# A routed-expert kernel: batch registers of the last group loaded earlier, additions chained by twos

## The chip, the cores and the metric

The kernel runs on one core of one Trainium2 chip. The metric is the device time of the kernel in microseconds; lower is better. Before the change three runs took 675.02, 675.02 and 675.72 us.

## What is computed

The reference has two residual stages on x, of shape 64 batches x 64 steps x 256 features, all in float32.

```python
x = x + _L0_cond_ref(x, cond, weight, bias)     # a gated recurrent cell, scanned over the 64 steps
x = x + _L1_cond_ref(x, cond, ...)              # a gated mixture of 4 experts, 2 for each batch

for e in range(E):                              # E = 4
    h = gelu(context_c @ ew1[e] + eb1[e])       # 256 -> 1024
    y = h @ ew2[e] + eb2[e]                     # 1024 -> 256
    out = out + w_be[:, e][:, None, None] * mask[e][None, :, None] * y
shared = gelu(context_c @ sw1 + sb1) @ sw2 + sb2
return out + shared
```

`w_be` is zero for the two experts that a batch did not choose. The mask takes steps 21 to 41 out of expert 1 and steps 0 to 20 out of expert 2. Which expert a batch goes to is known only while the kernel runs.

## The kernel before

**Stages.** The recurrent scan runs step by step; beside it TensorE works on the shared expert in groups of 8 steps (512 columns). When the scan is over, the gate is computed (`gate_means` to `gate_weights`), and from it two lists: `slot_b`, one row of batch numbers on partition 0, and `slot_w`, the weights. A group of the routed part takes 8 slots (experts 0 and 3, 64 steps each, 512 columns) or 10 slots (expert 1: 44 steps that are used, 440 columns, with step 21 set to zero by a memset; expert 2: 43 steps, 430 columns). Every group has 10 places in the list (`WIDE`). Places without a batch hold batch 0 with weight 0. Expert q of `ORDER` has groups `sv[q]` to `sv[q+1]`, with `sv` read from the chip (`group_bounds`); each expert has one group at least. With these inputs there are 15 groups: seven for expert 0 (from 348 us), one for expert 3 (from 498), six for expert 1 (from 520), one for expert 2 (from 635).

**One group.** Eight chunks of 128 hidden units. For each one TensorE does layer 1 (`hp`), ScalarE the gelu (L364, `g_f`) and the rounded copy (L369, `g_hi`), DVE the rest `g_lo = g_f - g_hi` (L458, `split_lo`), TensorE layer 2 (`zy`) with `g_hi` and, last, with `g_lo`. Layer 2 of chunk j comes behind layer 1 of chunk j + 2. Layer 2 of the last two chunks is interleaved with layer 1 of the next group (`turnover`). Every matmul is recorded at L775.

**What DVE does beside it.** When a group's layer 2 is complete, `weigh` (L671) adds the bias, multiplies by the slots' weights and writes `y_w`. During the next group `add_slots` loads batch numbers into registers (L686), two or three at a time, and adds each slot's part of `y_w` into `acc` at the address of its batch (L692). Each addition waits until the one before is complete: empty slots all point to batch 0, so neighbours can have the same address. In the first group of an expert the additions are those of the expert before (`add_prior`), and for the next expert's weights DVE makes the low parts of eight pieces (`piece_low`, L466). A piece comes by a DMA from SyncE (L225) into one of three staging buffers, ScalarE makes its high part (L375), DVE the low part, and only then SyncE may refill the buffer.

**The end.** The last expert's branch ends with the wait for all additions and `head_ready`, at which SyncE issues the output of steps 0 to 20 (L227). It stands ahead of the splits of chunks 6 and 7, behind each of which `batches` (L706) loads registers: 2, then 8 batch numbers of the same group. After the loop's last group `add_last` adds the ten slots from these registers, first for feature half k = 0, then for k = 1 (L718), and after each half SyncE issues that half's output for steps 21 to 63 (L230).

```python
bs = []
for j in range(common, NCH):
    split_lo(r + NG, j, n)
    bs += batches(r, len(bs), WIDE - 2 if bs else 2)
```

Of the kernel before, what the change touches and what calls it, by code (L numbers as in the profile page):

```python
# [9 lines left out]
ALU = mybir.AluOpType  # L10
# [4 lines left out]
B = 64  # L15
# [3 lines left out]
E = 4  # L19
HID = 1024  # L20
NCH = HID // P
GT = 8
NG = T // GT
QT = 4
SLOTS = 8
WIDE = 10
HEAD = T // 3
PROP = T - 2 * HEAD
MAXG = (2 * B + (SLOTS - 1) * E) // SLOTS + 1
NSLOT = MAXG * WIDE  # L30
PIECE = 512
# [7 lines left out]

RUNS = [(0, 1, T, T), (0, 2, 2 * HEAD, PROP), (HEAD, 1, T, T - HEAD), (0, 1, T, T)]  # L40
TOKS = [n * length for _, n, _, length in RUNS]
MASKED_EXPERT, MASKED_STEP = 1, HEAD
PER = [SLOTS if TOKS[e] == T else WIDE for e in ORDER[1:]]
NFULL = sum(p == SLOTS for p in PER)
assert PER == [SLOTS] * NFULL + [WIDE] * (E - NFULL)
assert PROP == HEAD + 1

# [5 lines left out]
C_IOTA = C_TRI + B  # L53
# [9 lines left out]
def cond_resid_kernel(nc, x, w0, w_exp, small, consts, out):  # L63
    ctx = ExitStack()
    with ctx:
        def sb(name, shape, dt=F32):
            return ctx.enter_context(nc.sbuf_tensor(name, shape, dt))
# [4 lines left out]
        def sem(name):  # L72
            return ctx.enter_context(nc.semaphore(name))
# [35 lines left out]
        con = sb("con", [P, C_END])  # L109
# [9 lines left out]
        slot_b = h_f[0:1].rearrange("p i k b -> p (i k b)")[:, 0:WIDE + NSLOT].bitcast(I32)  # L119
# [7 lines left out]
        gp, lists = zy[:, 0], zy[:, 1]  # L127
# [43 lines left out]
        sel_done, pos_mm, starts_done, pick_done, list_mm, batches_done = (  # L171
            sem(n) for n in ("sel_done", "pos_mm", "starts_done", "pick_done", "list_mm", "batches_done"))
# [3 lines left out]
        gather_done, yw_done, add_done = sem("gather_done"), sem("yw_done"), sem("add_done")  # L176
# [8 lines left out]
        def group_bounds(eng):  # L185

            eng.wait_ge(starts_done, 1)
            return [eng.value_load(starts[0:1, e:e + 1], min_val=0, max_val=MAXG) for e in range(E + 1)]

# [4 lines left out]
        def pieces_at(j):  # L194

            return [[], [0], [1], [2], [3], [4], [5], [6, 7]][j]

        def tokens_of(t, e, b):

            first, n, step, length = RUNS[e]  # L200
            v = t[..., first:first + n * length, bass.ds(b, 1)]
            if len(v.shape) == 5:
                v = v.rearrange("p s k (i t) b -> p (s k) i (t b)", i=n)
            else:
                v = v.rearrange("p k (i t) b -> p k i (t b)", i=n)
            return bass.AP(v.tensor, v.offset, [list(v.ap[0]), list(v.ap[1]), [step * B, n], [B, length]])
# [239 lines left out]
        def _(dve):  # L446
            count = [0]

            def link(ins):

                count[0] += 1
                ins.then_inc(dve_math, 1)
                dve.wait_ge(dve_math, count[0])

            def split_lo(g, j, n):
                c = g * NCH + j
                dve.wait_ge(ghi_done, c + 1)
                dve.tensor_tensor(g_lo[:, j % 2, 0:n], g_f[:, j % 2, 0:n], g_hi[:, j % 2, 0:n].bitcast(F32),  # L458
                                  ALU.subtract).then_inc(glo_done, 1)
# [101 lines left out]
            def gate_means():  # L561
# [5 lines left out]
                link(dve.tensor_scalar(agg[:, 0], agg[:, 0], 1.0 / T, None, ALU.mult))  # L567
                dve.tensor_scalar(agg[:, 1:3], agg[:, 1:3], 1.0 / (HEAD + PROP), None, ALU.mult).then_inc(agg_done, 1)

# [85 lines left out]
            gate_slots()  # L655
            shared_out(NG - 2, yp)
            dve.wait_ge(list_mm, 1)
            dve.tensor_copy(slot_b[0:1, WIDE:WIDE + NSLOT], lists[0:1, 0:NSLOT]).then_inc(batches_done, 1)
            dve.wait_ge(batches_done, 1)
            gather_first()  # L660
            gate_weights()
            sv = group_bounds(dve)

            def weigh(r, q):
# [15 lines left out]
                else:  # L680
                    dve.sem_inc(y_read, 1)

            def add_slots(r, q, slots):

                e, n = ORDER[q + 1], TOKS[ORDER[q + 1]]
                bs = nc.values_load_multi_w_load_instructions(slot_b[0:1, bass.ds(r * WIDE + slots[0], len(slots))], engines=(mybir.EngineType.DVE,), min_val=0, max_val=B - 1)[1]  # L686
                for s, b in zip(slots, bs):
                    if s == 0:
                        dve.wait_ge(y_read, r + NG)
                    dve.wait_ge(add_done, r * WIDE + s + 1)  # L690
                    dst = tokens_of(acc, e, b)
                    dve.tensor_tensor(dst, dst, y_w[:, :, s * n:(s + 1) * n].rearrange("p k (a n) -> p k a n", a=RUNS[e][1]),  # L692
                                      ALU.add).then_inc(add_done, 1 if s < PER[q] - 1 else WIDE - s)

            def slots_at(q, per, i):

                cuts = [0, 3, 6, 8, per] if q == E - 1 and per == WIDE else [min(2 * c, per) for c in range(NCH)]
                return list(range(cuts[i], cuts[i + 1])) if i + 1 < len(cuts) else []

            def add_prior(r, q, slots):  # L700

                add_slots(r, q - 1, slots)

            def batches(r, a, n):

                return nc.values_load_multi_w_load_instructions(  # L706
                    slot_b[0:1, bass.ds((r + 1) * WIDE + a, n)], engines=(mybir.EngineType.DVE,), min_val=0, max_val=B - 1)[1]

            def add_last(r, e, bs):

                n = TOKS[e]
                dve.wait_ge(y_read, r + NG + 1)
                for k in range(K):
                    for s in range(WIDE):
                        dve.wait_ge(add_done, (r + 1 + k) * WIDE + s + 1)
                        dst = tokens_of(acc[:, k:k + 1], e, bs[s])
                        src = y_w[:, k:k + 1, s * n:(s + 1) * n].rearrange("p k (a n) -> p k a n", a=RUNS[e][1])
                        dve.tensor_tensor(dst, dst, src, ALU.add).then_inc(add_done, 1)  # L718
                    dve.wait_ge(add_done, (r + 2 + k) * WIDE + 1)
                    dve.sem_inc(out_ready, 1)  # L720
# [7 lines left out]
            split_lo(NG, 1, n0)  # L728
            dve.wait_ge(weight_mm, 1)
            dve.tensor_copy(slot_w[:], lists[:, NSLOT:2 * NSLOT])  # L730
            for q in range(E):
                e = ORDER[q + 1]
                n = PER[q] * TOKS[e]
                with dve.Fori(sv[q], sv[q + 1]) as r:

                    common = NCH - 2 if q == E - 1 else NCH
                    with dve.If(sv[q] < r):
                        for j in range(2, common):
                            split_lo(r + NG, j, n)
                            if slots_at(q, PER[q], j - 2):  # L740
                                add_slots(r, q, slots_at(q, PER[q], j - 2))
                    with dve.Else():
                        for j in range(2, common):
                            split_lo(r + NG, j, n)
                            if q == E - 1 and slots_at(q, PER[q - 1], j - 2):
                                add_prior(r, q, slots_at(q, PER[q - 1], j - 2))
                            elif q and j > 2 and slots_at(q, PER[q - 1], j - 3):
                                add_prior(r, q, slots_at(q, PER[q - 1], j - 3))
                            if q < E - 1:
                                for m in (pieces_at(1) if j == 2 else []) + pieces_at(j):  # L750
                                    piece_low((q + 2) * NP + m)
                        if q == E - 1:
                            dve.wait_ge(add_done, (r + 1) * WIDE + 1)
                            dve.sem_inc(head_ready, 1)
                    bs = []
                    for j in range(common, NCH):
                        split_lo(r + NG, j, n)
                        bs += batches(r, len(bs), WIDE - 2 if bs else 2)
                    with dve.If(r + 1 < sv[q + 1]):
                        split_lo(r + NG + 1, 0, n)  # L760
                        weigh(r, q)
                        split_lo(r + NG + 1, 1, n)
                    with dve.Else():
                        nn = PER[q + 1] * TOKS[ORDER[q + 2]] if q < E - 1 else 0
                        if nn:
                            split_lo(r + NG + 1, 0, nn)
                        weigh(r, q)
                        if nn:
                            split_lo(r + NG + 1, 1, nn)
                        else:  # L770
                            add_last(r, e, bs)
        @block.tensor
        def _(pe):
            def mm(out_, lhsT, rhs, start, stop=False):
# [242 lines left out]
```

## Time and profile before

| | us |
|---|---|
| runs (median; lowest to highest) | 675.02; 675.02 to 675.72 |
| the profiled execution | 675.07 |
| its span | 673.17 |
| TensorE busy with matmuls | 641.2 (95%) |
| DVE busy | 413.9 (61%) |
| ScalarE busy | 311.7 (46%) |
| GpSimd busy | 256.1 (38%) |
| chain that ended last: share of TensorE, of DVE, of DVE's queue | 89%, 4%, 2% |

All times within the execution are counted from the span's start. A name such as DVEq or SPq is the sequencer of an engine: register steps, waits, branches and DMA issues, which are not counted as busy. The releaser in brackets behind an instruction is what ended the engine's idle time before it; "issue" is none that the profile shows.

### The profile page before, as it was taken

What the parts mean: (1) busy time and instruction counts of PE and PEld (TensorE: products, weight loads), DVE (VectorE), ACT (ScalarE), POOL (GpSimd) and SP (SyncE); (2) the same over time, 40 slices, a digit from 0 to 9 for tenths busy, and PEclk for the clock granted to TensorE, in tenths of its full rate; (3) what the DMA queues carried; (4) which work ended last, traced back from release to release, by engine and by line L of the source; (5) the groups of instructions that cost most, each with busy time, mean ns of one, the idle gap of its engine ahead of it and who ended that gap; (6) DMA issues with size and microseconds to landing.
All of it is one profiled execution on the core that took longest, in us unless ns stands there. A gap on an engine that the chain in (4) does not pass through costs nothing.

```text
span 673.2 us, 16856 instructions
## 1 busy us (share of the span) xinstructions
PE 641.2 (95%) x5708; PEld 550.4 (82%) x5708; DVE 413.9 (61%) x940; ACT 311.7 (46%) x521; POOL 256.1 (38%) x510
## 2 busy tenths in 40 slices
PE   7789999999999999999999999999999999999980
PEld 4678888888888888888778888888888999999970
DVE  5788866666656566677676554545457765555543
ACT  5445444334434343344556444454456755555530
POOL 1477754454545445333456123320333222333000
PEclk9999999999999999999999999999999999999995
DMA  7521100000000000000003000000003300000024
GB/s 263 195 65 51 61 2 2 0 0 0 0 0 0 0 0 0 1 2 1 1 1 124 1 0 0 0 0 0 0 1 107 98 0 0 0 0 0 0 83 168
DMA packets 7749, 20.71 MB, mean 31 GB/s; under 512 B 800, under 2 KB 1056, under 8 KB 7200
## 3 DMA queue, kind: packets, MB, share of 16 engines
q1 hardware_dynamic: 7424, 19.59, 8.3%
q10 hardware_dynamic: 288, 0.64, 0.3%
q8 instruction: 21, 0.34, 0.2%
q14 instruction: 16, 0.13, 0.1%
HBM read 16.03 MB, written 4.19 MB: 30 GB/s over the span
## 4 chain that ended last, share of the span: by engine, by line
PE 89%; DVE 4%; DVEq 2%; issue 1%; ACT 1%; DMA 1%; POOL 1%; SPq 0%; ACTq 0%
PE zy L775 54%; PE hp L775 35%; DMA acc<-in_x 1%; DVEq L706 1%; DVE acc L718 1%; DVEq L686 1%; DVE d_t L485 1%; ACT uc L352 1%; DVE d_t L483 0%; DVE acc L692 0%; DVE h_b L488 0%; DVE y_all L625 0%; POOL x_hl L255 0%; ACT g_hi L369 0%; DVEq L718 0%
## 5 line engine op out<-in xcount | busy, mean ns | idle before, releaser
L458 DVE TENSOR_TENSOR g_lo<-g_f,g_hi 128x512 fp32r<-128x512 f32 (+2 forms) x176 | 131.1, 745 | 124.1 <-ACT g_hi L369 118.6
L775 PE MATMUL zy<-g_hi,w_buf 128*128 128x512 f32 (+2 forms) x736 | 192.1, 383 | 0.0
L369 ACT ACTIVATE g_hi<-g_f 128x512 fp32r<-128x512 f32 (+2 forms) x184 | 112.9, 614 | 156.6 <-PE zy L775 156.5
L364 ACT ACTIVATE g_f<-hp,first 128x512 f32<-128x512 f32 (+2 forms) x184 | 123.3, 670 | 122.6 <-PE hp L775 117.4
L775 PE MATMUL hp<-shared_buf,w_buf 128*128 (+1 forms) x720 | 173.6, 376 | 0.4 <-issue 0.4
L775 PEld LDWEIGHTS zy<-g_hi,w_buf 128*128 128x128 f32 x736 | 135.3, 188 | 19.9
L775 PEld LDWEIGHTS hp<-shared_buf,w_buf 128*128 128x128 f32 x720 | 135.0, 188 | 19.9 <-issue 1.1
L775 PEld LDWEIGHTS zy<-h_b,y_all 128*128 128x128 bf16 x3072 | 93.7, 98 | 25.3 <-issue 14.8
L775 PE MATMUL zy<-g_lo,w_buf 128*128 128x512 f32 (+2 forms) x368 | 110.4, 381 | 0.0
L775 PE MATMUL zy<-h_b,y_all 128*128 128x64 bf16 x3072 | 102.3, 193 | 8.2 <-DVE h_b L488 7.7
L775 PE MATMUL hp<-x_hl,w_buf 128*128 (+1 forms) x384 | 103.3, 404 | 0.9 <-POOL x_hl L255 0.9
L692 DVE TENSOR_TENSOR acc<-acc,y_all 128x128 f32 (+1 forms) x124 | 50.0, 403 | 55.9 <-issue 47.0
L330 POOL CAST shared_buf<-x_hl x126 | 82.2, 701 | 0.0
L775 PEld LDWEIGHTS zy<-g_lo,w_buf 128*128 128x128 f32 x368 | 69.0, 188 | 12.1 <-DVE g_lo L458 0.2
L775 PEld LDWEIGHTS hp<-x_hl,w_buf 128*128 128x128 f32 x384 | 67.7, 189 | 13.2 <-POOL x_hl L255 1.5
L326 POOL TENSOR_TENSOR turn<-turn 128x1 f32<-128x1 f32 x14 | 3.5, 249 | 188.7 <-PE hp L775 188.7
L252 POOL TENSOR_TENSOR x_hl<-acc,first 128x128 f32 (+1 forms) x57 | 25.6, 450 | 114.1 <-DVE first L492 114.1
L775 PE MATMUL zy<-x_hl,shared_buf 128*128 (+1 forms) x384 | 56.4, 285 | 0.6 <-POOL x_hl L280 0.6
L775 PEld LDWEIGHTS zy<-x_hl,shared_buf 128*128 128x128 f32 x384 | 52.8, 189 | 4.8 <-DVE zy L521 1.1
L352 ACT ACTIVATE uc<-zy 128x256 f32<-128x256 f32 x64 | 24.6, 384 | 51.6 <-PE zy L775 51.6
L671 DVE SCALAR_TENSOR_TENSOR y_all<-zy,first,uc 128x512 f32 (+2 forms) x30 | 20.1, 711 | 23.5 <-PE zy L775 17.0
L466 DVE TENSOR_TENSOR w_buf<-stage,w_buf 128x512 fp32r<-128x512 f32 x40 | 32.9, 835 | 0.0
(118 smaller groups left out, 416.8 us busy)
## 6 DMA issues: line engine op xcount, KB each, us to landing
stage<-in_w_exp SPq DMA_DIRECT2D x40, 256.0 KB, 2.9
out_y<-acc SPq DMA_DIRECT2D x2, 1376.0 KB, 5.0
acc<-in_x SPq DMA_DIRECT2D x1, 2048.0 KB, 7.8
acc<-in_x SPq DMA_DIRECT2D x1, 1536.0 KB, 9.9
out_y<-acc SPq DMA_DIRECT2D x1, 1344.0 KB, 5.1
acc<-in_w SPq DMA_DIRECT2D x1, 512.0 KB, 4.6
acc<-in_x SPq DMA_DIRECT2D x1, 512.0 KB, 6.8
acc<-in_w ACTq DMA_DIRECT2D x1, 512.0 KB, 5.6
```

The lines of the kernel that those rows point to most:

```text
L252: pool.tensor_tensor(hi, a, h_f[:, 1 - i % 2], ALU.add).then_inc(x1_hi, 1)
L330: last = pool.tensor_copy(dst, tokens_of(x_hl, e, bs[s]))
L352: act.activation(uc[:], zb[:, buf, :, :, i % QT, :], ACT.Tanh).then_inc(tanh_done, 1)
L364: act.activation(g_f[:, j % 2, 0:n], hp[j % 2][:, 0:n], ACT.Gelu_apprx_tanh, bias=par[:, S_B1 + e * NCH + j:S_B1 + e * NCH + j + 1]).then_ ...
L369: act.activation(g_hi[:, j % 2, 0:n], g_f[:, j % 2, 0:n], ACT.Copy).then_inc(ghi_done, 1)
L458: dve.tensor_tensor(g_lo[:, j % 2, 0:n], g_f[:, j % 2, 0:n], g_hi[:, j % 2, 0:n].bitcast(F32), ALU.subtract).then_inc(glo_done, 1)
L466: dve.tensor_tensor(w[:, 1, c:c + PIECE], stage[:, n % RING], w[:, 0, c:c + PIECE].bitcast(F32), ALU.subtract).then_inc(piece_done, 1)
L485: dve.scalar_tensor_tensor(out=d_t[:], in0=uc[:, 0], scalar=1.0, in1=d_t[:], op0=ALU.add, op1=ALU.mult).then_inc(q_done, 1)
L671: dve.scalar_tensor_tensor(out=y_w[:, k, 0:per * n].rearrange("p (s n) -> p s n", n=n), in0=y_bank(r)[k][:, 0:per * n].rearrange("p (s n) ...
L686: bs = nc.values_load_multi_w_load_instructions(slot_b[0:1, bass.ds(r * WIDE + slots[0], len(slots))], engines=(mybir.EngineType.DVE,), mi ...
L692: dve.tensor_tensor(dst, dst, y_w[:, :, s * n:(s + 1) * n].rearrange("p k (a n) -> p k a n", a=RUNS[e][1]), ALU.add).then_inc(add_done, 1 ...
L775: return pe.matmul(out_, lhsT=lhsT, rhs=rhs, start=start, stop=stop, skip_group_check=True)
```

## The change

There are four edits, all on DVE.

1. The ten batch registers of the last group are loaded earlier: numbers 0 to 4 behind the loop of the first expert in `ORDER`, 5 to 9 behind the loop of the second. The address comes from `sv[E]`, the number of groups. `batches` and its two calls go.
2. With that, the last expert's chunks 6 and 7 are split inside the two branches like all the others, and `head_ready` comes behind them.
3. From the third slot on an addition waits only for the additions up to the last but one (`order_add`). In `add_last` the first addition of the second half waits for nothing of its own (the wait for the whole first half stands before it).
4. So that neighbouring empty slots differ, the list's copy to `slot_b` becomes a maximum with the pattern 0, 1, 0, 1 (from `con`): empty places point to batch 0 or 1 by parity. A batch 0 that was chosen is always the first slot of an expert and stays 0.

```diff
+EARLY = [0, 5, 10]
...
-            dve.tensor_copy(slot_b[0:1, WIDE:WIDE + NSLOT], lists[0:1, 0:NSLOT]).then_inc(batches_done, 1)
+            parity = con[0:1, C_IOTA:C_IOTA + 2].unsqueeze(1).to_broadcast([1, NSLOT // 2, 2])
+            dve.tensor_tensor(slot_b[0:1, WIDE:WIDE + NSLOT].rearrange("p (a n) -> p a n", n=2),
+                              lists[0:1, 0:NSLOT].rearrange("p (a n) -> p a n", n=2), parity, ALU.max).then_inc(batches_done, 1)
...
+            def order_add(done, s):
+
+                dve.wait_ge(add_done, done + (s if s < 2 else s - 1))
+
...
-                    dve.wait_ge(add_done, r * WIDE + s + 1)
+                    order_add(r * WIDE + 1, s)
...
-            def batches(r, a, n):
-
-                return nc.values_load_multi_w_load_instructions(
-                    slot_b[0:1, bass.ds((r + 1) * WIDE + a, n)], engines=(mybir.EngineType.DVE,), min_val=0, max_val=B - 1)[1]
...
-                        dve.wait_ge(add_done, (r + 1 + k) * WIDE + s + 1)
+                        if s or k == 0:
+                            order_add((r + 1 + k) * WIDE + 1, s)
...
+            last_bs = []
...
-                    common = NCH - 2 if q == E - 1 else NCH
                     with dve.If(sv[q] < r):
-                        for j in range(2, common):
+                        for j in range(2, NCH):
                             split_lo(r + NG, j, n)
...
                         if q == E - 1:
                             dve.wait_ge(add_done, (r + 1) * WIDE + 1)
                             dve.sem_inc(head_ready, 1)
-                    bs = []
-                    for j in range(common, NCH):
-                        split_lo(r + NG, j, n)
-                        bs += batches(r, len(bs), WIDE - 2 if bs else 2)
...
-                            add_last(r, e, bs)
+                            add_last(r, e, last_bs)
+                if q + 1 < len(EARLY):
+                    last_bs += nc.values_load_multi_w_load_instructions(
+                        slot_b[0:1, bass.ds(sv[E] * WIDE + EARLY[q], EARLY[q + 1] - EARLY[q])], engines=(mybir.EngineType.DVE,),
+                        min_val=0, max_val=B - 1)[1]
```

## Rows read from the trace of the kernel before

**Rows 1.** Section 1 of the page: busy us (share of the span) xinstructions.

```profile
PE 641.2 (95%) x5708; PEld 550.4 (82%) x5708; DVE 413.9 (61%) x940; ACT 311.7 (46%) x521; POOL 256.1 (38%) x510
```

**Rows 2.** Stretches: length, busy us of each engine (instructions), granted clock, DMA share, GB/s.

```profile
500.00:541.00 41.00, 41.00 (x196) 36.40 (x195) 32.19 (x52) 28.79 (x49) 13.33 (x20) 1.00 0.27 85
...
634.00:653.00 19.00, 18.98 (x98) 17.84 (x96) 9.28 (x21) 8.87 (x15) 0.00 (x0) 1.00 0.09 37
653.00:673.00 20.00, 0.00 (x0) 0.00 (x0) 5.87 (x22) 0.00 (x0) 0.00 (x0) 0.55 0.42 176
```

**Rows 3.** Timeline 630 to 674: start us, us, engine line op out<-in xcount [idle before].

```profile
636.04 0.56 PE L775 MATMUL zy<-g_lo,w_buf 128*128 128x440 f32 x2
...
637.05 1.26 DVE L671 SCALAR_TENSOR_TENSOR y_all<-zy,first,uc 128x440 f32 x2 [1.51 <-PE zy L775]
...
650.12 0.61 SPq L227 DMA_DIRECT2D out_y<-acc  x1
...
651.66 0.61 DVE L458 TENSOR_TENSOR g_lo<-g_f,g_hi 128x430 fp32r<-128x430 f32 x1 [0.77 <-ACT g_hi L369]
...
652.32 0.66 PE L775 MATMUL zy<-g_lo,w_buf 128*128 128x430 f32 x2
658.59 1.24 DVE L671 SCALAR_TENSOR_TENSOR y_all<-zy,first,uc 128x430 f32 x2 [6.32 <-issue]
660.16 3.60 DVE L718 TENSOR_TENSOR acc<-acc,y_all 128x43 f32 x10 [0.34 <-DVEq L681]
663.85 4.43 SPq L230 DMA_DIRECT2D out_y<-acc  x2
```

**Rows 4.** Lines L706, L686, L644: queue operations, count, ns min/median/max, first and last start us.

```profile
L706 DVEq FUSED_REGOPS  x12: 64/183/190, 650.3 to 657.6; - x12
...
L706 DVEq TENSOR_LOAD <-first x2: 536/2200/3864, 650.4 to 651.8; - x2
...
L686 DVEq TENSOR_LOAD <-first x61: 521/529/752, 373.1 to 647.9; - x61
...
L644 DVEq TENSOR_LOAD <-first x1: 866/866/866, 333.4 to 333.4; - x1
```

**Rows 5.** Chain that ended last, 638 to 674 (start us, us, what), and line L718.

```profile
644.99 0.04 DVEq L690
...
645.17 0.35 DVE acc L692
...
659.17 0.67 DVE y_all L671
...
L718 DVE TENSOR_TENSOR acc<-acc,y_all x20: 230/232/232, 660.2 to 667.6; 128x43 f32 x20
```

**Rows 6.** Stretches of one us in the tail, and the output's row of section 6.

```profile
652.00:653.00 1.00, 0.98 (x5) 0.40 (x3) 0.27 (x1) 0.00 (x0) 0.00 (x0) 1.00 1.05 425
...
665.00:666.00 1.00, 0.00 (x0) 0.00 (x0) 0.47 (x3) 0.00 (x0) 0.00 (x0) 0.50 1.05 440
...
668.00:669.00 1.00, 0.00 (x0) 0.00 (x0) 0.00 (x0) 0.00 (x0) 0.00 (x0) 0.50 0.46 184
...
out_y<-acc SPq DMA_DIRECT2D x2, 1376.0 KB, 5.0
```

**Rows 7.** Timelines of the turnovers at 502 and 524, DVE, PE and ACT.

```profile
503.52 0.69 DVE L458 TENSOR_TENSOR g_lo<-g_f,g_hi 128x512 fp32r<-128x512 f32 x1 [0.71 <-ACT g_hi L369]
...
507.58 0.62 PE L775 MATMUL zy<-g_lo,w_buf 128*128 128x512 f32 x2
...
524.58 0.62 DVE L458 TENSOR_TENSOR g_lo<-g_f,g_hi 128x440 fp32r<-128x440 f32 x1 [0.39 <-ACT g_hi L369]
525.11 1.28 DVE L466 TENSOR_TENSOR w_buf<-stage,w_buf 128x512 fp32r<-128x512 f32 x2
...
528.11 0.56 PE L775 MATMUL zy<-g_lo,w_buf 128*128 128x440 f32 x2
...
529.59 0.63 ACT L375 ACTIVATE w_buf<-stage 128x512 fp32r<-128x512 f32 x1 [0.25 <-DMA stage<-in_w_exp]
```

More of the change, by code:

```diff
@@ L742, in _ @@
                     with dve.Else():
-                        for j in range(2, common):
+                        for j in range(2, NCH):
                             split_lo(r + NG, j, n)
[L745 to L748, printed above, removed]
+                            i = j - 2 if q == E - 1 else j - 3
+                            if q and i >= 0 and slots_at(q, PER[q - 1], i):
+                                add_prior(r, q, slots_at(q, PER[q - 1], i))
                             if q < E - 1:
```

## The prediction

> **What bounds the kernel now.** I read the busy shares first: TensorE has matmuls in 95% of the span, the vector engine (DVE below) in 61% [rows 1]. Then the table of stretches, since an average hides the end: from 634 to 653 us TensorE has no gap to speak of (18.98 of 19.00), and from 653 to 673 it does nothing at all, while DVE is busy for 5.87 of 20 us and the DMA engines for 0.42 of the time [rows 2]. So there are two regimes. Before 653 only what stalls TensorE costs time. After it some 20 us are a serial tail, in which each microsecond taken from its chain comes off the total.
>
> The timeline of that tail [rows 3] gives the chain: the last g_lo split at 651.66, the last two matmuls until 652.98, then nothing on any engine until DVE's weighting (L671) at 658.59, ten additions from 660.16 to 663.76, the first output transfer's issue at 663.85, ten more additions, and the second issue, which ends at 668.28. The gap of 6.3 us before 658.59 is the register loads of line 706: a load of eight values that held DVE's queue for 3.86 us, and ten register steps of 0.18 us with an assertion each [rows 4]. They were queued in front of the weighting, whose operands were ready at 653.
>
> **The time that the sum starts from.** The profiled execution took 675.07 us with a span of 673.17; 1.9 us lie around it, which I take as unchanged. The median of the runs is 675.02, so both are the same to 0.05 us. A difference of 0.2% (1.35 us) is about what a measurement of this kernel can tell from none.
>
> **Part 1: the loads leave the tail.** The weighting will start as soon as the last matmul is seen. How long that takes is read from the group before: matmuls end at 636.60, L671 starts at 637.05, so 0.45 us [rows 3]. New start: 652.98 + 0.45 = 653.43 in place of 658.59, a gain of 5.16 us. The first of the two loads also stood in front of the last split (651.66), and TensorE's last pair of matmuls waited for that split a little. I take 0.1 us for it, between 0 and 0.2 (an estimate: a split takes 0.61, ended at 652.27, and the matmuls started at 652.32). Part 1 is -5.26 us.
>
> **Part 2: additions by twos.** Now every addition waits for the one before: ten take 3.60 us, and one takes 0.232 [rows 3, 5], so they start (3.60 - 0.23) / 9 = 0.374 apart. After the change the second still waits for the first; from the third on each waits for the last but one only, so what spaces them is the larger of three things. Half the chained distance, 0.374 / 2 = 0.19. The engine itself: the two weightings overlap, for they take 1.24 us together although one lasts 0.67, which would make 1.34 end to end [rows 3, 5]. The sequencer: from the register step before an addition to its start there are 645.17 - 644.99 = 0.18 us [rows 5], and such a step can begin only after the addition before is sent off, so I take 0.21. Ten then take 0.37 + 8 x 0.21 + 0.23 = 2.28 us: a gain of 1.3 us for the first half, between 0 (nothing overlaps) and 1.5 (0.18 apart).
>
> The other half's additions get shorter in the same way, but what follows them is a transfer. One half holds 1376 KB, 1.41 MB, and lands 5.0 us after its issue. Its data flow at 440 GB/s in the second after 665, which makes 3.2 us, say 3.4 with the ends. In the second from 668 the rate falls to 184 GB/s [rows 6]: that is the gap between the halves, since the second issue (about 667.9) comes 4.1 us after the first (663.85), later than the first's data need. With shorter additions the issues are some 2.8 us apart, the second half waits for the first one's data, and 4.1 - 3.4 = 0.7 us go. Any further speed of the second ten additions is worth nothing. Between 0 and 0.9; I take 0.7.
>
> The chains by twos inside the loops (L692) lie beside TensorE's matmuls, which have no gaps there [rows 2]. They are priced at nothing; DVE gets 0.1 to 0.2 us of air per pair. If that cover were gone, they would gain and not lose.
>
> **Part 3: the loads come back at two turnovers.** Behind the first expert's loop (near 502.3 us) and behind the second's (near 523.8) DVE's queue now loads five registers each. A load of two takes 0.53 us, of three 0.75 (both from L686's range 521 to 752), of eight 0.87 where nothing else goes on [rows 4]; for five I take 0.8. With an address step of 0.1 and five steps of about 0.28 (step, assertion and the gaps between) each place costs DVE's queue 2.35 us, between 2.1 and, if a load were to hang as the one at 651.8 did, 5.4.
>
> What stands behind them in the queue: the split of the group's third chunk, then two weight splits (L466), then the additions. At the second place the chunk's split moves from 524.58 to about 526.9 and ends at 527.5; TensorE wants it for the pair of matmuls at 528.11 [rows 7]. Margin 0.6 us. At the first place it moves from 503.52 to 505.45, ends at 506.1, wanted at 507.58: margin 1.5. So the matmuls cover both, and I price them at nothing. The weight splits are a second path. They free the staging buffers, SyncE refills those, and ScalarE's L375 already waits 0.25 us for a transfer at 529.59 [rows 7]; with the weight splits at 525.11 done 2.3 us later it comes at 531.9, and ScalarE, in order, holds the next gelu until 532.5. Following it through the group, TensorE needs that gelu's output for a matmul block about 5 us after 528.11, near 533.3, and it is there at 533.2. The margin is thin but the sum is zero; if the load is longer by a microsecond, TensorE loses about that, once.
>
> **Part 4: small edits.** The list copy becomes a maximum with a 0/1 pattern: a few hundredths on a 1 x 200 instruction, in front of DVE's gather, which ended before TensorE's own register loads did. Nothing. The head's output is issued after the last split and not before the last two: from 650.12 to about 651.4. Its 3.5 us of data then run until 656.2, before the first half's issue near 657.2. Nothing, as long as those two do not meet. They run beside the weighting and the additions; the additions beside the first half's transfer took the same 0.232 as the rest, so I expect no slowing.
>
> **The sum.** -5.26 - 1.3 - 0.7 = -7.26. 675.07 - 7.26 = **667.8 us**.
>
> **Rivals.**
> *The additions do not overlap* (10%). The chain by twos gives nothing, because DVE starts one operation only when the one before has left it. Then the ten still take 3.6 us, the issues stay 4.1 apart, and Part 1 alone remains: 675.07 - 5.26 = 669.8. Against it: the two weightings that overlap, though what they save is 0.1 us only. [...]
>
> *The stall was not the load's own* (7%). The 3.86 us at 651.78 are 3 us more than the same load of eight took elsewhere, and lie exactly where the head's output leaves at 425 GB/s [rows 4, 6]. If it was DVE's queue as a whole that stood (fetching its program, say), it will stand again, now in front of the weighting: part 1 shrinks by 3, to 670.8. For it: nothing else in DVE's queue ran then. Against: the additions beside the halves' transfers run on.
>
> *The turnover leaks* (7%). TensorE waits 0.3 to 2 us at 524 to 541, by either path of part 3: 668.1 to 669.8.
>
> *Slower* (2%). [...]
>
> *Nothing changes* (2%): some other wait ends at 658.6. Only line 706 stands there, so I see no candidate.
>
> **How the numbers follow.** The forecast has 72%. Its own range, from the bounds of parts 1 and 2, is 667.0 to 668.8. The range given reaches up to take in the first rival and most of the third, to 670.1, and leaves out 11%. Faster 0.96, the same 0.02, slower 0.02.
>
> **What would show it.** In the profile after: no register load between the last split and the weighting, L671 at 653.4; ten additions in 2.3 us, with waits only between the first two; first half issued at 657.2, second about 2.8 later, no dip in the rate between them; the clock at full until then. TensorE without gaps from 500 to 545, the third split at 526.9 and ScalarE's wait for the staging transfer grown from 0.25 to about 2 us. A gap on TensorE at 524 to 541 means part 3 is wrong; additions still 0.37 apart, part 2; an idle DVE from 653 on, part 1.

## The result and the profile after

The changed kernel takes 669.46 us (median of 4 runs, 669.27 to 669.49) against 675.02 before: a ratio of 0.9914, with a 95% interval from 0.9897 to 0.9932. The forecast was 667.8 with a range from 667.0 to 670.1. The profiled execution took 669.49 us with a span of 667.59, so 1.9 us lie around the span as before. On two other chips, in the experiments below, the same kernel took 669.02 and 669.10.

The tail after, in the timeline of all engines; these lines answer to [rows 3]:

```profile
652.21 0.61 DVE L459 TENSOR_TENSOR g_lo<-g_f,g_hi 128x430 fp32r<-128x430 f32 x1 [1.70 <-ACT g_hi L370]
652.38 0.61 SPq L228 DMA_DIRECT2D out_y<-acc  x1
...
653.28 0.55 PE L777 MATMUL zy<-g_lo,w_buf 128*128 128x430 f32 x2
654.29 1.24 DVE L674 SCALAR_TENSOR_TENSOR y_all<-zy,first,uc 128x430 f32 x2 [1.48 <-PE zy L777]
655.86 2.28 DVE L721 TENSOR_TENSOR acc<-acc,y_all 128x43 f32 x10 [0.34 <-DVEq L684]
658.23 3.26 SPq L231 DMA_DIRECT2D out_y<-acc  x2
```

The 6.3 us of idle DVE are gone. The matmuls end at 653.83 and the weighting starts 0.46 us later, released by them and by nothing else. The ten additions take 2.28 us, to the hundredth what the forecast had. The head's output leaves beside the weighting and slows nothing (the weighting takes 1.24 us, as before): its last packet ends at 657.14, ahead of the first half's issue.

Three things are not as forecast. The first is at the very end. Stretches of one us while the two halves leave; they answer to [rows 6] (columns: length, busy us of PE, PEld, DVE, ACT and POOL, granted clock, DMA share, GB/s):

```profile
661.00:662.00 1.00, 0.00 (x0) 0.00 (x0) 0.06 (x1) 0.00 (x0) 0.00 (x0) 0.50 0.86 352
662.00:663.00 1.00, 0.00 (x0) 0.00 (x0) 0.00 (x0) 0.00 (x0) 0.00 (x0) 0.50 1.22 515
...
665.00:666.00 1.00, 0.00 (x0) 0.00 (x0) 0.00 (x0) 0.00 (x0) 0.00 (x0) 0.50 0.64 264
666.00:667.00 1.00, 0.00 (x0) 0.00 (x0) 0.00 (x0) 0.00 (x0) 0.00 (x0) 0.50 0.03 11
```

And the output's row of the page, where the halves landed after 5.0 us before:

```profile
out_y<-acc SPq DMA_DIRECT2D x2, 1376.0 KB, 5.6
```

The dip between the halves is gone, as forecast. But after 666 there are still 11 GB/s, a DMA share of 0.03 over one us. In the trace's packets all but two have ended by 665.92, and these two end one behind the other, at 666.31 and 666.72. From the first half's issue to the end of the span it takes 667.59 - 658.23 = 9.36 us, where before it took 673.17 - 663.85 = 9.32. The 0.7 us did not come.

The second is the turnover that [rows 7] show. The early loads in the view of their line (count: ns min/median/max, first and last start us):

```profile
L771 DVEq TENSOR_LOAD <-first x2: 629/910/1191, 503.0 to 524.4; - x2
```

And the timeline around the second, for DVE, ScalarE and TensorE:

```profile
527.89 0.62 DVE L459 TENSOR_TENSOR g_lo<-g_f,g_hi 128x440 fp32r<-128x440 f32 x1 [3.12 <-ACT g_hi L370]
...
532.06 0.63 ACT L376 ACTIVATE w_buf<-stage 128x512 fp32r<-128x512 f32 x1 [2.14 <-DMA stage<-in_w_exp]
...
538.69 1.36 PE L777 MATMUL hp<-shared_buf,w_buf 128*128 x6
...
539.76 0.64 ACT L376 ACTIVATE w_buf<-stage 128x512 fp32r<-128x512 f32 x1 [2.11 <-DMA stage<-in_w_exp]
...
541.41 1.46 PE L777 MATMUL hp<-shared_buf,w_buf 128*128 x6 [0.15 <-issue]
...
543.90 1.36 PE L777 MATMUL hp<-shared_buf,w_buf 128*128 x6
```

Layer 1 of consecutive chunks is 2.40 us apart where nothing is lost (538.02 and 540.42 with moved loads, below). Here it is 2.72 and then 2.49, so TensorE lost 0.41 us. The first five registers took 0.63 us, the second five 1.19, and ScalarE waited twice for a refilled staging buffer, 2.1 us each.

The third is a matter of this execution. Stretches of one us from 28 on:

```profile
28.00:29.00 1.00, 0.00 (x0) 0.00 (x0) 0.93 (x4) 0.77 (x3) 0.58 (x2) 1.00 0.47 133
29.00:30.00 1.00, 0.89 (x20) 0.89 (x21) 0.83 (x5) 0.00 (x0) 0.00 (x0) 0.67 0.37 129
30.00:31.00 1.00, 1.00 (x23) 1.00 (x21) 0.84 (x2) 0.00 (x0) 0.68 (x1) 0.50 0.06 16
31.00:32.00 1.00, 1.00 (x16) 1.00 (x14) 0.00 (x0) 0.26 (x1) 0.94 (x3) 0.50 0.10 25
```

TensorE had stood still for 1.67 us, from 27.44 to 29.11, and its granted clock was 0.50 from 29.33 to 32.74. Ahead of this place TensorE was 0.11 us earlier than in the profile before, behind it 0.52 to 0.54 later. Two more profiles of the same kernel show the dip once and miss it once. The standstill alone does not explain it: TensorE stands still for the same 1.67 us in the profile before, whose clock stayed at 1.00:

```profile
28.00:29.00 1.00, 0.00 (x0) 0.00 (x0) 0.93 (x3) 0.88 (x3) 0.69 (x2) 1.00 0.36 131
29.00:30.00 1.00, 0.78 (x24) 0.76 (x24) 0.86 (x4) 0.00 (x0) 0.00 (x0) 1.00 0.36 131
```

The sum, from one profile to the other, in starts: the weighting moved by 658.59 - 654.29 = 4.30 us. The loads were worth 5.16, and the last split 0.13 (from its first matmul to its last the routed part took 311.76 us before and takes 311.63 where nothing is lost, see below). Against that the routed part starts 0.58 later (341.80 after 341.22), most of it by the clock, and 0.41 went to the turnover. The first ten additions gave 1.32 and the end gave 0: 5.6 of span.

### The profile page after: what moved, and what is told of

Read it like the earlier page. It is cut to its first block, busy times and chain, and to the rows that moved or that the text cites. A ratio compares the mean times of both kernels' runs of the same rounds, so it can differ in the third digit from the quotient of the medians.

```text
span 667.6 us, 16841 instructions
## 1 busy us (share of the span) xinstructions
PE 642.3 (96%) x5708; PEld 551.7 (83%) x5708; DVE 409.5 (61%) x940; ACT 311.4 (47%) x521; POOL 257.6 (39%) x510
## 4 chain that ended last, share of the span: by engine, by line
PE 92%; DVE 3%; DMA 1%; ACT 1%; issue 1%; POOL 1%; DVEq 0%; SPq 0%; ACTq 0%
PE zy L777 56%; PE hp L777 36%; DMA acc<-in_x 1%; ACT uc L353 1%; DVE d_t L486 1%; DVE d_t L484 0%; DVE acc L721 0%; DVE h_b L489 0%; DVE y_all L626 0%; POOL x_hl L256 0%; ACT zy L348 0%; DVE w_buf L467 0%; DVE gs L608 0%; POOL acc L254 0%; DVEq L721 0%
## 5 line engine op out<-in xcount | busy, mean ns | idle before, releaser
L331 POOL CAST shared_buf<-x_hl x126 | 83.8, 715 | 0.0
L699 DVE TENSOR_TENSOR acc<-acc,y_all 128x128 f32 (+1 forms) x124 | 46.6, 417 | 47.2 <-issue 45.2
L275 POOL TENSOR_TENSOR seg<-seg,acc (+1 forms) x64 | 32.0, 500 | 0.6
```

The source lines that it names most:

```text
L275: pool.tensor_tensor(sg, sg, a, ALU.add).then_inc(seg_done, 1)
L331: last = pool.tensor_copy(dst, tokens_of(x_hl, e, bs[s]))
```

## The experiments

All times are medians of 4 or 5 runs, with the kernel before run beside them: it took 675.52 us beside the first four, 675.43 on the chip of the two paddings and of the strict second half, and 675.06 on that of the last three. The intervals of the ratios are some 0.3% wide (2 us), so differences of less than a microsecond are read from durations inside the profiles.

### What the loads and the chains are worth alone

The loads moved early, every addition chained to the one before, the list copied as it was:

```diff
-                dve.wait_ge(add_done, done + (s if s < 2 else s - 1))
+                dve.wait_ge(add_done, done + s)
...
-                        if s or k == 0:
+                        if True:
```

> The changed kernel without its chains: the registers are loaded early, but every addition waits for the one before and the list is copied as it was. My theory of where 669.46 comes from: the early weighting is worth 4.3 us here (5.2 less a clock dip at 30 us and a leak at the turnover at 541), the short chain of the first ten additions 1.3, and the second ten nothing, because the gap of 0.75 us that goes from between the two output transfers comes back as a DMA engine that ends 0.8 us after the others. So loads only: k = 0 takes 3.6 us, gap back, straggler hidden: 669.5 + 1.3 = 670.8. Rival, the second ten do count by 0.7: 671.5. Rival, the additions never overlapped: 669.5.

Measured: 671.15 us (670.86 to 671.57), ratio 0.9936 (0.9923 to 0.995). The first ten additions in DVE's timeline, then ScalarE's waits from 522 to 545 (us in total, times, longest us):

```profile
656.20 3.60 DVE L719 TENSOR_TENSOR acc<-acc,y_all 128x43 f32 x10 [0.34 <-DVEq L682]
```

```profile
ACT w_buf L376 <- DMA stage<-in_w_exp: 5.0, 2, 2.8
```

The additions are back at 3.60 us, so the third reading (they never overlapped) falls. The time lies between the other two, but the profile decides: from the first half's issue (659.88) to the end (669.25) it takes 9.37 us, as with the short chain. What is extra is at the turnover. ScalarE's waits grew from 4.3 us in the changed kernel to 5.0, and the routed part, from its first matmul at 341.22 to the last one's end at 654.17, takes 312.95 us, where 311.6 is the length without any loss (below). So the chains inside the loops, which I had priced at nothing, give DVE back time behind the early loads. Without them the leak is 1.3 us in this one profile; in the six profiles that have them, and five registers loaded at 524, it is 0.4 to 0.9.

The other half alone, with the list's 0/1 pattern that it needs: the loads stay in the tail.

```diff
-                    dve.wait_ge(add_done, r * WIDE + s + 1)
+                    dve.wait_ge(add_done, r * WIDE + 1 + (s if s < 2 else s - 1))
...
-                        dve.wait_ge(add_done, (r + 1 + k) * WIDE + s + 1)
+                        if s or k == 0:
+                            dve.wait_ge(add_done, (r + 1 + k) * WIDE + 1 + (s if s < 2 else s - 1))
```

> The kernel before with the chains by twos and the parity list only; the loads stay in the tail. First ten additions 2.3 in place of 3.6 us: -1.3. The three pairs inside the last group also end earlier, so the head's output is issued about 0.7 us earlier, and the load of eight registers, if it waits for that transfer, ends 0.7 earlier: together 675.0 - 2.0 = 673.0. If the load's length has nothing to do with the transfer it keeps 3.86 us and the time is 673.7. If shorter second ten count too, 0.7 less in both.

Measured: 672.71 us (672.64 to 672.85), ratio 0.9959 (0.9946 to 0.9973). The tail's loads in the view of their line, then the head's issue in SyncE's timeline:

```profile
L708 DVEq TENSOR_LOAD <-first x2: 540/1909/3278, 649.4 to 651.3; - x2
```

```profile
649.04 0.61 SPq L227 DMA_DIRECT2D out_y<-acc  x1
```

The head's output leaves 1.08 us earlier than before (650.12), and the load of eight, which starts at 651.28, ends at 654.56 and not at 655.65: 1.09 earlier. The load ends with the transfer: in both profiles 0.76 us behind its last packet (653.80 here, 654.89 before). 1.3 us from the additions and 1.1 from the load that ended sooner make the 2.4 by which the span is shorter (673.17 to 670.80).

### Why the load of eight took 3.86 us

```diff
-                        if q == E - 1:
-                            dve.wait_ge(add_done, (r + 1) * WIDE + 1)
-                            dve.sem_inc(head_ready, 1)
                     bs = []
                     for j in range(common, NCH):
                         split_lo(r + NG, j, n)
                         bs += batches(r, len(bs), WIDE - 2 if bs else 2)
+                    if q == E - 1:
+                        dve.wait_ge(add_done, (r + 1) * WIDE + 1)
+                        dve.sem_inc(head_ready, 1)
```

> The kernel before with one thing moved: the wait for all additions and head_ready stand behind the register loads of the tail and not in front of the last two splits. Theory: the load of eight took 3.86 us because the output of the head left SBUF at 425 GB/s beside it. Without that it takes about 0.9, the weighting starts 3 us earlier and the time is 672.0. Rival: a load of eight at this address takes 3.9 anyway (an unaligned one on GpSimd's queue takes 1.8): 675.0, or 673.0 if it takes 1.8.

Measured: 672.75 us (672.67 to 673.15), ratio 0.9961 (0.9947 to 0.9975). The loads' line, and the weighting in DVE's timeline:

```profile
L706 DVEq TENSOR_LOAD <-first x2: 536/1190/1844, 649.9 to 651.2; - x2
```

```profile
656.18 1.24 DVE L671 SCALAR_TENSOR_TENSOR y_all<-zy,first,uc 128x430 f32 x2 [4.46 <-issue]
```

Both readings had a part of it. Without the outgoing transfer beside it the same load takes 1.84 us: 2.02 of the 3.86 were the transfer's, and 1.84 is its own length at this address. Moving the wait and the signal behind the loads, with nothing else changed, takes 2.4 us off the span: 2.0 from the load's length, the rest because the splits no longer stand behind the wait and the load starts 0.55 us earlier (651.23).

### Where the loads may stand

The first five are loaded ahead of the loops, the second five behind the first expert's; nothing at 524.

```diff
-                if q + 1 < len(EARLY):
-                    last_bs += nc.values_load_multi_w_load_instructions(
...
+            last_bs = list(early(0))
...
+                if q == 0:
+                    last_bs += early(1)
```

> The changed kernel with its two loads of five at other places: the first before the loops, the second behind the first expert's loop; none at the turnover at 524 us. Theory: TensorE lost 0.38 us at 541 because the load of five there (1.19 us, not 0.8) made the first weight splits 3.3 us late and the refilled staging buffers with them. Without it TensorE has no gap at 541: 669.46 - 0.4 = 669.1. Rival: the first group, which also fetches pieces, leaks the same at 350 to 370: 669.5. If the loss at 541 came from the pairs of additions or from the profile's chance, 669.5 too, with the gap still at 541.

Measured: 668.49 us (668.40 to 668.54), ratio 0.9897 (0.9882 to 0.9912). The changed kernel was run again on another chip:

> The changed kernel once more, on the chip of the runs beside it: 669.4 to 669.5. Its profile tells whether the clock dip at 29 to 33 us (0.5 us on TensorE) belongs to the kernel or to chance, and whether one DMA engine again ends 0.8 us behind the others at the end.

Measured: 669.02 us (668.69 to 669.28), ratio 0.9905 (0.989 to 0.992). Layer 1 on TensorE near 540 in the timeline of this repetition, then of the kernel with moved loads, then the loads of the latter:

```profile
538.05 1.36 PE L777 MATMUL hp<-shared_buf,w_buf 128*128 x6
...
541.20 1.47 PE L777 MATMUL hp<-shared_buf,w_buf 128*128 x6 [0.24 <-issue]
```

```profile
538.02 1.36 PE L781 MATMUL hp<-shared_buf,w_buf 128*128 x6
...
540.42 1.36 PE L781 MATMUL hp<-shared_buf,w_buf 128*128 x6
```

```profile
L736 DVEq TENSOR_LOAD <-first x2: 643/913/1183, 350.2 to 502.3; - x2
```

The repetition lost 0.75 us in one step (3.15 in place of 2.40) and has no clock dip; the first profile had the dip and a smaller leak. With moved loads the spacing is 2.40 all through, and the weighting starts at 653.21. The leak is 0.4 to 0.9 us, and the clock dip comes and goes with the execution. The first group takes its five registers without loss: its layer 1 steps are spaced as in the kernel before, and the routed part takes 311.63 us. The changed kernel was not run beside this one, so the 0.5 us between the two medians is not a measure of the leak.

The five numbers that took 1.19 us take 1.18 here, 22 us earlier, and the others stay at 0.63 and 0.64. So the length goes with the address in the list and not with the moment. GpSimd's queue shows the same in every profile, here that of the changed kernel; it loads whole groups, eight or ten numbers each, at places ten apart:

```profile
L323 POOLq TENSOR_LOAD <-first x14: 572/1436/2270, 346.0 to 595.1; - x14
```

The seven loads of eight took 1.84, 0.59, 1.83, 0.58, 1.83, 0.57 and 1.83 us in their order, and the seven of ten alternate between 1.03 to 1.05 and 2.27. One more kernel asks both things again:

```diff
-EARLY = [0, 5, 10]
+EARLY = [0, 8, 10]
```

> The changed kernel with eight registers loaded behind the first expert's loop and two behind the second's, in place of five and five. Two things are asked. The length of a load: the first five took 0.63 us and the second five 1.19 wherever they stood, and all lengths seen fit 0.30 + 0.22 for each further register, but less where the address starts on 16 bytes and four or more are taken. The first eight start on such an address: 0.87 us, where the eight of the tail took 1.84 without a transfer beside them. Rival: the length goes by the count alone, 1.84. And the leak: at 524 the queue now holds two registers, 1.1 us in place of 2.6, so the weight splits are 1.5 us earlier and TensorE has no gap at 541: as loads_moved, 668.5. If the leak comes from anything else there: 669.0 to 669.5. At 502 the queue holds 3.1 us against a margin of some 3.8: no gap.

Measured: 668.84 us (668.55 to 670.56), ratio 0.9902 (0.9886 to 0.9919). Its profiled execution is the one of 670.56, which had two clock dips (at 11 and at 31 us) and is late by 2 us before the routed part begins; from there on it can be read. The loads, and layer 1 on TensorE:

```profile
L771 DVEq TENSOR_LOAD <-first x2: 530/568/607, 504.5 to 525.9; - x2
```

```profile
537.76 1.36 PE L777 MATMUL hp<-shared_buf,w_buf 128*128 x6
...
540.16 1.36 PE L777 MATMUL hp<-shared_buf,w_buf 128*128 x6
```

No gap, and the routed part takes 311.63 us, as with moved loads: the leak hangs on the queue time at 524 (here two registers in 0.53 us, in the changed kernel five in 1.19). (The median, 668.84, is not clear of the changed kernel's 669.10 on this chip.) Eight registers took 0.61 us, three times faster than the eight in the tail (1.84) and less than I expected (0.87).

### What holds the end

The second ten additions chained strictly again:

```diff
-                            order_add((r + 1 + k) * WIDE + 1, s)
+                            dve.wait_ge(add_done, (r + 1 + k) * WIDE + 1 + (s if s < 2 or k else s - 1))
```

> The changed kernel with the second half's ten additions chained strictly, the first half's by twos. The second output transfer is issued 1.3 us later, 4.1 after the first. If one late DMA engine (it carries an 8 KB program fetch between the two transfers) sets the end anyway, the gap of 0.75 us between the transfers comes back on the other fifteen engines only and costs nothing: 669.5. If the gap really counts, as I had predicted: 670.2.

Measured: 669.03 us (668.87 to 669.53), ratio 0.9909 (0.9894 to 0.9924), against 669.02 for the changed kernel on the same chip. The two issues in SyncE's timeline, then stretches of one us:

```profile
657.77 4.42 SPq L231 DMA_DIRECT2D out_y<-acc  x2
```

```profile
662.00:663.00 1.00, 0.00 (x0) 0.00 (x0) 0.00 (x0) 0.00 (x0) 0.00 (x0) 0.50 0.45 184
...
666.00:667.00 1.00, 0.00 (x0) 0.00 (x0) 0.00 (x0) 0.00 (x0) 0.00 (x0) 0.50 0.01 0
```

The dip between the halves is back (184 GB/s), the second issue is 1.2 us later, and the time is the same. So the short chain of the second ten additions buys nothing in the changed kernel. What takes its place is a program fetch. The DMA queues from 658 on, in the changed kernel (packets, MB, share of 16 engines):

```profile
q1 hardware_dynamic: 288, 2.82, 67.7%
q14 instruction: 1, 0.01, 0.2%
```

One instruction fetch of 8 KB starts at 662.79 and takes 0.31 us. The packet that starts where it ends, at 663.10, takes 0.76 us where the others take 0.41, and two ahead of it (661.25 and 661.80) take 0.54 and 0.57. The packets do not name their DMA engine; that these are on one engine is read from ends and starts that join, and from the two late packets at the end. DVE stops once in the second ten additions (0.38 us idle before 659.75), and I take that for the place where its program goes from one block to the next, a block being what one fetch brings; how many instructions that is, no run shows. To move the block's end, instructions that are never executed were put in:

```diff
                     with dve.If(sv[q] < r):
+                        if q == E - 1:
+                            for _ in range(60):
+                                dve.memset(gs[:, 65:66], 0.0)
                         for j in range(2, NCH):
```

> The changed kernel with 60 small instructions put into a branch of the last expert that is never taken with these inputs. They run nowhere; they shift the addresses of DVE's last instructions by 60. [...] With 60 more the block ends before the first half's additions, the fetch rides with the head's transfer, which nobody waits for: 669.46 - 0.8 = 668.7, all sixteen DMA engines ending together. Rival: the late engine is late for a reason of its own (the fetch is another engine's or goes along wherever): 669.5.

Measured: 668.44 us (668.08 to 668.69), ratio 0.9898 (0.9882 to 0.9913), 0.58 less than the changed kernel on the same chip (669.02, 668.69 to 669.28). The DMA queues from 652 to 658:

```profile
q1 hardware_dynamic: 272, 1.38, 56.4%
q14 instruction: 1, 0.01, 0.7%
```

From 658 on, with no instruction queue:

```profile
q1 hardware_dynamic: 288, 2.82, 67.4%
```

The last stretches, and the second ten additions:

```profile
665.00:666.00 1.00, 0.00 (x0) 0.00 (x0) 0.00 (x0) 0.00 (x0) 0.00 (x0) 0.50 0.43 176
666.00:667.00 1.00, 0.00 (x0) 0.00 (x0) 0.00 (x0) 0.00 (x0) 0.00 (x0) 0.50 0.00 0
```

```profile
658.24 2.29 DVE L721 TENSOR_TENSOR acc<-acc,y_all 128x43 f32 x10 [0.24 <-DVE acc L721]
```

The fetch rides with the head's transfer, the second ten additions run without a stop (2.29), and from the first half's issue to the end it takes 666.55 - 658.09 = 8.46 us and not 9.36. No packet takes longer than 0.45 us there. From one profiled execution to the other, 669.28 to 668.45, that accounts for the difference; the medians show 0.58 of it. That the second half's short chain is worth something once the fetch is away is not tested by itself: no run had the padding with the strict chain.

> The same with 108 instructions, so that the block ends only behind the last addition and no fetch of DVE's falls on either output transfer: 668.7 by the theory of the fetch, 669.5 by the rival. [...]

Measured: 669.22 us (669.12 to 669.69), ratio 0.9913 (0.9899 to 0.9926): this one missed. The additions run through (2.28 us for the second ten), but the queues from 658 on still show one fetch, now at 662.94, and from the issue to the end it takes 9.34 us. The 108 rested on my estimate of how many instructions one fetch brings, and no run shows that number. What the runs show is where the last fetch falls: at 653.50 with 60 instructions, ahead of the first half's issue (658.09), and at 662.94 with 108, 4.95 us behind it (657.99). The one padding that helped put the fetch before the first half, not just behind the stop that was seen.

### Both finds together

> Both finds together: the loads at the places of loads_moved and the 60 instructions of padding. The leak (0.4 to 0.9 us) and the late DMA engine (0.8 us) are separate stretches, so they add: 668.49 - 0.8 = 667.7, the tail without a gap from 652.8 on and all sixteen engines ending within 0.3 us. If one hides the other: 668.4.

Measured: 667.57 us (667.39 to 667.76), ratio 0.9885 (0.9868 to 0.9901), the fastest of all. The changed kernel beside it:

> The changed kernel beside the two, for a comparison on one chip: 669.0 to 669.5.

Measured: 669.10 us (668.82 to 669.79). The difference is 1.53 us, and the ranges are apart. Between the two profiles 0.88 is the fetch, 0.37 the leak and 0.37 a clock dip in that of the changed kernel, so the leak and the fetch are most of it. DVE's and SyncE's part of the tail:

```profile
653.25 1.24 DVE L674 SCALAR_TENSOR_TENSOR y_all<-zy,first,uc 128x430 f32 x2 [1.47 <-PE zy L784]
654.82 2.28 DVE L721 TENSOR_TENSOR acc<-acc,y_all 128x43 f32 x10 [0.34 <-DVEq L684]
657.19 2.87 SPq L231 DMA_DIRECT2D out_y<-acc  x2
```

This is the timeline that the prediction described for the changed kernel (weighting at 653.4, first issue at 657.2), 0.2 us from its 667.8.

The time from the first half's issue to the end of the span, in the profiles before and after and in nine of the experiments:

| kernel | second issue after the first, us | fetch on the halves | issue to end, us |
|---|---|---|---|
| before | 4.08 | yes | 9.32 |
| after | 2.92 | yes | 9.36 |
| loads only | 4.25 | yes | 9.37 |
| twos only | 2.91 | yes | 9.35 |
| head late | 4.09 | yes | 9.33 |
| second ten strict | 4.07 | yes | 9.32 |
| loads moved | 2.91 | yes | 9.34 |
| eight and two | 2.92 | yes | 9.36 |
| 108 instructions | 2.52 | yes | 9.34 |
| 60 instructions | 2.52 | no | 8.46 |
| moved and 60 | 2.53 | no | 8.46 |

## Why the prediction came out as it did

**Part 1, the loads out of the tail.** Right in mechanism and in size: 5.16 us, 0.46 from the last matmul to the weighting. The head's transfer did not meet the first half's. In the kernel with moved loads, where nothing else is lost, the weighting starts 5.38 us earlier than before (658.59 to 653.21), which is the 5.16, 0.13 for the last split, and 0.09 by which the routed part happened to start earlier. The rival of a stall that was the queue's own fell: with no load in the tail there is no stop in front of the weighting.

**Part 2, the additions.** The first ten: 2.28 us forecast, 2.28 measured. The overlap is real but small: from the fourth addition on they start 0.217 us apart at 0.23 each. What the chain by twos saves is above all the wait from one addition to the next, 0.374 apart when each waits for the one before. The agreement to the hundredth is in part luck, for the 0.21 of the forecast was a guess above a reading of 0.18, and one step of 0.145, for the third addition, brings the mean of eight down to it. With the loads as early, the same ten took 3.60 us where each waits for the one before (the kernel with the loads only) and 2.28 by twos. The rival (669.8) is out for that reason, though the measured time lies near it.

The second ten are the term that failed. "4.1 - 3.4 = 0.7 us go" took the transfers as one stream. They are some 16 at once (packets of 11 KB that take 0.41 us each, at 440 GB/s), and the last of them ends the kernel. My reading of the packets' times is that the stream with the program fetch had used the gap between the halves to catch up: before, with a fetch at 668.37 (0.31 us) and single packets of 0.56 and 0.59 us, the last twenty packets still end within 0.16 us of each other, and with the gap closed the last two end 0.4 and 0.8 us behind the others. The gain is 0 with the fetch in its place, and with both the gap and the fetch gone 0.9 (9.32 to 8.46).

**Part 3, the loads at the turnovers.** Two steps failed. The load's size: 0.8 us taken between lengths of two, three and eight, 0.63 and 1.19 measured. And the path's end: it was followed to 533 and no further. I had written that a load longer by a microsecond costs TensorE about that; 0.4 longer came with a loss of 0.4 to 0.9. The path was the one named: late weight splits, late refill, ScalarE's wait for the transfer 2.1 us (forecast about 2), and the output of the gelu late near 540. I placed the tight spot at 533 and it held there: ScalarE went on at 532.06, which is 531.5 in the times of the profile before (the routed part starts 0.58 later here), against 531.9 in the forecast. It gave way at the next turnover, where two pieces stand in a row (ScalarE's second wait, until 539.76). No run had a load of 0.8 us at 524, so how much of the leak is the size and how much would have been there anyway stays open; with the two registers of 0.53 us it is nothing. And the chains inside the loops were priced at nothing on the ground that they lie beside the matmuls. With the loads in the queue that is no longer so: they hold the leak to 0.4 to 0.9 us in place of 1.3.

**Part 4.** Nothing, as forecast.

**The rivals.** The leak, held at 7%, is what happened, together with the forecast's mechanism; it was a term to be added and not a case of its own. The slower case did not come near: the load at 524 took 1.19 us and not some 3 us more than the 0.8 forecast, and TensorE's granted clock stayed at 1.00 from 32.74 until 657.38, behind its last matmul.

**The number.** 669.46 lies in the range that was given, but outside the forecast's own (667.0 to 668.8); the upper end had been set for two rivals, and one of them is refuted. Of the 1.66 us above 667.8 some 0.9 are the program fetch, which no rival named, and 0.4 to 0.9 the leak. So the number is in part luck. The clock dip is seen in the profile and not in the times: the four runs have mean granted clocks of 0.990 to 0.993 and lie within 0.22 us. The forecast's own range was not what its bounds give either: with 5.16 to 5.36, 0 to 1.5 and 0 to 0.9 taken off 675.07 it would be 667.3 to 669.9.

What stays open is how a load's length hangs on its address. Eight numbers took 0.61 us at the list's place 150, 1.84 at place 152 and 0.87 at place 10; five took 0.63 at 150 and 1.19 at 155; two always 0.52 to 0.56. That fits 0.3 us and 0.22 for each further number, but for five and more at some places. The list has four bytes a number, so GpSimd's groups are 40 bytes apart, and fast and slow in turn is what a boundary of 16 bytes would give. That is an estimate from these loads; the boundary was not tried by itself, and it does not tell 0.61 at place 150 from 0.87 at place 10. At how many numbers it begins, four in the expectation, is an estimate too: no load had four, and the two of three (0.75) stood at places 140 and 143, where GpSimd's load of ten at 140 was a slow one (2.27).

## What to carry to other kernels

Register loads with a runtime address belong where their queue has nothing urgent behind it (5.16 us were gained here), away from transfers that leave SBUF (3.86 us beside one, 1.84 without), and at a place of the list that is seen to load fast (0.61 against 1.84 for eight); their cost at a new place is set by the tightest chain behind them, which here ran through a weight split, a refill and a third engine before it took 0.4 to 0.9 us from TensorE. When the gap between two transfers at the end of a program is closed, look at which packets end last: one instruction fetch among them ate the gain here (9.36 us from issue to end with it, 8.46 without). A chain by twos asks that neighbours never share an address, which the pattern in the empty places ensures here, and takes ten short additions from 3.60 to 2.28 us.

## What the runs showed of the hardware that I had not expected

- A load of eight registers ran 2.0 us longer (3.86 against 1.84) beside an outgoing transfer of 1344 KB at 425 GB/s, and ended 1.09 us earlier when that transfer was issued 1.08 us earlier. Loads of two beside incoming transfers (0.54 at 506.4, with 258 GB/s) were not longer.
- The place in the list set a load's length: 0.61 against 1.84 us for eight numbers on DVE's queue, and 0.57 and 1.83 in turn on GpSimd's.
- One instruction fetch of 8 KB among the packets of two transfers of 1.41 MB put off the end by 0.9 us (9.36 against 8.46). Sixty instructions that never run moved the fetch to 653.50 and took that away.
- TensorE stands still for 1.7 us once between 27 and 31 us in all thirteen profiles. In three of them its granted clock then fell to 0.5, in two of three of the changed kernel, which cost 0.4 to 0.6 us; in ten it stayed at 1.00.
